# A gated block with a selective scan and a mixture of experts: the stage up to the first scan rearranged

## The reference

```
x    : (4, 256, 256)   ctx : (4, 256, 128)   E = 8 experts, top 2, M = 512
# part 1: a selective state space model, DI = 256 channels, DS = 16 states, DR = 8
xi    = in_proj_w @ ctx                       # per batch, channels x time
xc    = depthwise causal convolution, 4 taps, of xi;   u = silu(xc + conv_b)
x_dbl = x_proj_w @ u  -> dt_lo (8 rows), B (16 rows), C (16 rows)
delta = softplus(dt_proj_w @ dt_lo + dt_proj_b);       A = -exp(A_log)
state = state * exp(delta * A) + (delta * u) * B ;     y = sum over states(state * C) + D * u
y     = y * silu(layernorm(x))                # layernorm(x)[channel, time] stands as z
x     = x + tanh(g_xattn) * transpose(y)
# part 2: routed mixture of experts on 1024 tokens
x     = x + tanh(g_ffn) * moe(layernorm(x))   # softmax over the best two of 8 logits
```

## Time and profile before

| | |
|---|---|
| median of 3 runs | 315.19 us (313.74 to 315.58) |
| the profiled execution | 316.63 us, its span 314.9 us |
| busy in the span | PE 266.2, DVE 230.8, ACT 179.8, POOL 177.5 us |
| first scan begins | 39.81 us into the span |
| last scan ends, routing, first expert product | 161.2, then to 189.5 us |
| mean granted TensorE clock | 0.92 |

### The profile page before, as it was taken

One profiled execution on the slowest core, in us unless ns is written; L12 is line 12 of the kernel. 1 busy time (PEld: TensorE's weight loads), 2 busy tenths in 40 slices (PEclk: granted clock), 3 DMA queues, 4 the chain that ended last, 5 costly groups with the idle time before them and its releaser, 6 DMA issues.

```text
span 314.9 us, 4621 instructions
## 1 busy us (share of the span) xinstructions
PE 266.2 (85%) x1139; PEld 176.7 (56%) x1140; DVE 230.8 (73%) x423; ACT 179.8 (57%) x335; POOL 177.5 (56%) x159
## 2 busy tenths in 40 slices
PE   3957569869977998898799398999999999999970
PEld 3522133224332533463547276889889898898860
DVE  2775997999889999999887993565655656556540
ACT  1396477767566677557482852474564655646540
POOL 5000337997899899999675033246455464554331
PEclk9988558999999999999879857999999999999985
DMA  6599400000000000001069511042332432423312
GB/s 199 184 370 387 153 1 0 0 3 0 0 0 1 0 3 0 0 0 68 2 200 323 210 37 34 17 69 39 63 59 41 67 47 53 67 35 65 35 18 33
DMA packets 18911, 22.70 MB, mean 72 GB/s; under 512 B 2624, under 2 KB 14062, under 8 KB 18894
## 3 DMA queue, kind: packets, MB, share of 16 engines
q1 hardware_dynamic: 13312, 16.39, 15.1%
q0 software_dynamic: 4416, 6.03, 12.0%
q10 hardware_dynamic: 1166, 0.08, 0.2%
HBM read 17.38 MB, written 5.11 MB: 71 GB/s over the span
## 4 chain that ended last, share of the span: by engine, by line
PE 58%; DVE 19%; issue 9%; POOL 4%; ACT 4%; DMA 3%; POOLq 1%; SPq 0%; DVEq 0%; ACTq 0%
PE PZ L976 11%; PE PD L940 11%; PE PU L940 10%; PE PY L779 10%; DVE states L1116 5%; DVE states L1122 4%; POOL hC L403 3%; PE PY L962 3%; DMA xs<-in_x 3%; PE PU L768 2%; DVE W_lo L1213 2%; PE PY L738 2%; PE PZ L933 1%; PE PU L917 1%; PE PZ L827 1%
## 5 line engine op out<-in xcount | busy, mean ns | idle before, releaser
L403 POOL TENSOR_TENSOR hC<-states,WO 128x512 f32<-128x512 f32 x64 | 80.8, 1274 | 21.8 <-PE PY L779 14.7
L1122 DVE TENSOR_TENSOR_SCAN states<-PD,states 128x512 f32<-128x512 f32 x64 | 77.4, 1210 | 1.0 <-ACT PD L577 1.0
L779 PE MATMUL PY<-hC,ident 128*128 128x512 f32 x128 | 71.2, 644 | 6.0 <-POOL hC L403 5.9
L438 POOL DMA_INDIRECT out<-lg,y_at x23 | 36.4, 1584 | 54.5 <-ACT lg L670 49.0
L577 ACT ACTIVATE PD<-WO,Aneg 128x510 f32<-128x510 f32 x64 | 43.9, 689 | 22.2 <-DVE states L1122 18.0
L1359 DVE TENSOR_TENSOR WO_lo<-WO,WO_hi 128x512 fp32r<-128x512 f32 x46 | 29.8, 688 | 34.5 <-ACT WO_hi L663 33.9
L663 ACT ACTIVATE WO_hi<-WO 128x512 fp32r x46 | 26.5, 624 | 48.5 <-PE PZ L976 46.8
L1116 DVE TENSOR_TENSOR states<-PU,WO 128x512 f32<-128x512 f32 x64 | 42.8, 670 | 4.8 <-POOL hC L403 3.1
L425 POOL DMA_INDIRECT hC<-x_rows,x_at x23 | 23.2, 1008 | 27.2 <-DVE x_at L1329 14.9
L779 PEld LDWEIGHTS PY<-hC,ident 128*128 128x128 f32 x128 | 23.0, 200 | 22.4 <-POOL hC L403 15.6
L394 POOL TENSOR_TENSOR W_lo<-W,W_hi 128x512 fp32r<-128x512 f32 x23 | 29.2, 1275 | 0.0
(11 more groups left out here) (226 smaller groups left out, 509.7 us busy)
## 6 DMA issues: line engine op xcount, KB each, us to landing
W<-in_L_ffn_w SPq DMA_DIRECT2D x16, 512.0 KB, 10.9
WO<-in_L_ffn_wo SPq DMA_DIRECT2D x8, 512.0 KB, 5.7
xs<-in_x SPq DMA_DIRECT2D x1, 1024.0 KB, 8.3
out<-xs SPq DMA_DIRECT2D x2, 512.0 KB, 3.3
x_rows<-u SPq DMA_DIRECT2D x2, 512.0 KB, 5.3
early<-in_ctx SPq DMA_DIRECT2D x1, 512.0 KB, 4.3
hC<-x_rows,x_at POOLq DMA_INDIRECT x23, 2.8
out<-lg,y_at POOLq DMA_INDIRECT x23, 3.8
```

The lines of the kernel that those rows point to most:

```text
L403: pool.tensor_tensor(hC[:, n % 2, :], states[:, n % RING, :], C_rep[:, pair % C_RING, :], ALU.mult).then_inc(hc_done, 1)
L438: pool.indirect_dma_start(out=out, out_offset=bass.IndirectOffsetOnAxis(ap=y_at[:, s:s + 1], axis=0), in_=y_tile[s % 2], in_offset=None, c ...
L779: pe.matmul(PY[:, h, :], ident[:, :], hC[:, n % 2, :], start=False, stop=(m == DS - 1)).then_inc(y_done, 1)
L1122: dve.tensor_tensor_scan(states[:, n % RING, :], DEC[n % 2], states[:, n % RING, :], 0.0, ALU.mult, ALU.add).then_inc(scan_done, 1)
```

## The change

Five things, in one edit. The layout: batches' tokens and channels are loaded with two neighbouring rows per partition ("(p r)" and "(p h)" for "(r p)" and "(h p)"), so that DMAs have pieces twice as long; PE then reads and writes some operands with stride 2 (`x_cols`, `z_cols`, `x2`), and `cols` is loaded straight instead of being turned. x comes in two halves, statistics too. DMAs move between the SP and ACT queues; W1 is loaded whole before W0.

`u`: only quarter 1 (`CONV`) still has the four scaled products; quarters 0, 2 and 3 have one product (`channels`) and taps, whose first is ACT's (`start_taps`) and whose other three DVE's (`taps`). dt_proj is folded with the dt rows of x_proj into `dt_w` (two products with 8 rows), so that `delta_raw(c)` is two 128-row products from u itself, and no dt_lo is copied.

Roots are exp(-0.5 ln(var)) on ACT, with no Sqrt and no reciprocal. Eight products of the identity stand ahead of PE's first work. `silu_z` of the second half's four blocks moves behind the last scan.

The order: delta quarter 0 is finished first and scan 0 runs ahead of quarter 1's delta and du; `delta_raw(2)`, `x_dbl(1)`, `delta_raw(3)`, `rows_hi(1)` and `rows_lo(1)` move behind the first scans. Dropped lines that the new order replaces are left out below where the section above names them.

```diff
-        XI = [bank[i] for i in (2, 4)]
-        XD = [bank[i][0:BC_LO + 2 * DS, :] for i in (5, 4)]
+        XI = {(0, 0): bank[0], (1, 0): bank[2], (1, 1): bank[5]}
+        CONV = bank[1]
         DRAW = [bank[i] for i in (6, 7, 6, 7)]
...
+            sp.dma_start(ctx_sb.rearrange("p (b r) d -> p b r d", r=2), ctx_1024.rearrange("b (p r) d -> p b r d", p=P)).then_inc(ld["ctx"], 16)
...
-            def softplus_base(c):
-                pool.wait_ge(relu_ok, c + 1)
...
+            pool.wait_ge(relu_act, 1)
+            pool.wait_ge(rest_ok, 2)
+            pool.tensor_tensor(sp_relu[1], sp_relu[1], sp_rest[1], ALU.subtract).then_inc(base_pool, 1)
...
+            act.dma_start(convw[:, :, :], conv_w.rearrange("(p h) k -> p h k", p=P)).then_inc(ld["convw"], 16)
+            act.dma_start(xproj_sb[:, :], x_proj_w).then_inc(ld["small"], 16)
+            act.dma_start(dtw_sb[:, :, :], dt_proj_w.rearrange("(p h) r -> p h r", p=P)).then_inc(ld["small"], 16)
...
+            def start_taps(q, h):
+
+                act.wait_ge(xi_ps, 2 * q + h - (1 if q else 0) + 1)
+                act.activation(u[:, q, h, :], XI[q, h], ACT.Copy, scale=convw[:, h, DC - 1:DC]).then_inc(first_tap, 1)
...
+                act.wait_ge(stats_ok, (q + 1) * (2 * QBLK + 1))
...
+                act.wait_ge(ln_var, q + 1)
+                act.activation(rstd[:, 0, cut], std[:, 0, cut], ACT.Exp, scale=-0.5).then_inc(rstd_ok, 1)
...
+            start_taps(0, 0)
+            act.wait_ge(smallT_ps, 1)
+            act.activation(dtwT[:, :, :].rearrange("r h e -> r (h e)"), bank[3][0:DR, P:3 * P], ACT.Copy).then_inc(dtwT_ok, 1)
+            start_taps(1, 0)
+            root_first(0)
+            act.preload_act_table_set("silu_and_others")
+            start_taps(1, 1)
+            act.wait_ge(dt_w_made, 1)
+            act.activation(dt_w.rearrange("p h e -> p (h e)"), dt_w_ps, ACT.Copy).then_inc(dt_w_ok, 1)
             for h in range(2):
...
-            for i in range(2):
-                silu_z(i)
             silu_u(0)
-            for i in range(2, 7):
-                silu_z(i)
-            for c in range(1, 2 * NQ):
-                silu_u(c)
-            silu_z(7)
-            act.preload_act_table_set("natural_log_exp_and_others")
-            act.wait_ge(ld["small"], 16 * 7)
-            act.activation(Aneg[:, :, :], Aneg[:, :, :], ACT.Exp).then_inc(Aexp_ok, 1)
+            act.wait_ge(nmr_ok, 1)
+            silu_z(0)
+            silu_z(1)
+            silu_u(1)
+            silu_z(2)
+            silu_z(3)
+            silu_u(2)
+            silu_u(3)
+            act.wait_ge(ld["gates"], 32)
+            act.activation(tg[:, :], gates[:, :], ACT.Tanh).then_inc(tanh_ok, 1)
...
+                    if n == ROOT_AT:
+                        root(0)
...
+                act.activation(std[:, 1, cut], vare[:, 1, cut], ACT.Ln).then_inc(ln_var2, 1)
+                act.wait_ge(ln_var2, q + 1)
+                act.activation(rstd[:, 1, cut], std[:, 1, cut], ACT.Exp, scale=-0.5).then_inc(rstd2_ok, 1)
...
+            act.preload_act_table_set("natural_log_exp_and_others")
+            magnitude(0)
+            exponent(0)
+            logarithm(0)
             rows_hi(0)
-            rows_hi(1)
-            magnitude(0)
+            act.wait_ge(ld["A"], 16)
+            act.activation(Aneg[:, :, :], Aneg[:, :, :], ACT.Exp).then_inc(Aexp_ok, 1)
             magnitude(1)
-            exponent(0)
             exponent(1)
-            logarithm(0)
-            logarithm(1)
             act.wait_ge(Aneg_ok, 1)
             act.wait_ge(dec_clear, 2)
-            decay(0, 2)
+            decay(0, 1)
+            positive(1)
+            logarithm(1)
+            decay(1, 2)
+            rows_hi(1)
+            root_first(1)
+            decay(2, 3)
             positive(2)
-            decay(2, 3)
-            positive(3)
             decay(3, 4)
             magnitude(2)
             decay(4, 5)
-            magnitude(3)
-            decay(5, 6)
             exponent(2)
             plus_one(2)
-            decay(6, 8)
+            decay(5, 9)
+            logarithm(2)
+            positive(3)
+            decay(9, 10)
+            magnitude(3)
+            decay(10, 12)
             exponent(3)
             plus_one(3)
-            decay(8, 11)
-            logarithm(2)
-            decay(11, 13)
+            decay(12, 16)
             logarithm(3)
-            decay(13, NT)
+            decay(16, NT)
             act.wait_ge(exp_done, NT)
...
+            act.preload_act_table_set("silu_and_others")
+            for i in (QBLK, QBLK + 2, QBLK + 1, QBLK + 3):
+                silu_z(i)
+            act.preload_act_table_set("natural_log_exp_and_others")
             act.wait_ge(b_ps, NT // 2)
...
+            pe.wait_ge(consts, 2)
+            for _ in range(8):
+                pe.matmul(bank[3][:, 0:P], ident[:, :], ident[:, :], start=True, stop=True)
...
+            pe.wait_ge(tapw_ok, DC)
...
+            pe.wait_ge(ctxT_ok, 2)
+            channels(0, 0)
+            pe.wait_ge(ctxT_act, 1)
+            channels(1, 0)
+            pe.wait_ge(ld["small"], 16 * 2)
             for h in range(2):
-                pe.wait_ge(tapw_ok, DC * (h + 1))
-                for k in range(DC):
...
+            channels(1, 1)
+            pe.wait_ge(dtwT_ok, 1)
...
-            def delta_raw(q):
-
-                pe.wait_ge(dt_ok, q + 1)
+            def delta_raw(c):
...
+                q, to = divmod(c, 2)
                 for h in range(2):
-                    if q:
-                        pe.wait_ge(abs_ok, h + 1)
-                    pe.matmul(DRAW[2 * q + h], dtwT[:, h, :], dt_lo[:, q, :], start=True, stop=True).then_inc(draw_ps, 1)
-
-            pe.wait_ge(small_ok, 4)
-            pe.wait_ge(u_ok, 2)
+                    pe.wait_ge(u_ok, 2 * q + h + 1)
+                    mm = pe.matmul(DRAW[c], dt_w[:, h, to * P:(to + 1) * P], u[:, q, h, :], start=(h == 0), stop=(h == 1))
+                mm.then_inc(draw_ps, 1)
+
+            pe.wait_ge(dt_w_ok, 1)
+            delta_raw(0)
+            pe.wait_ge(small_ok, 3)
             x_dbl(0)
-            pe.wait_ge(u_ok, 4)
-            x_dbl(1)
-            delta_raw(0)
+            delta_raw(1)
...
+                x2 = PZ[r][:, :].rearrange("p (l e h) -> p l h e", l=2, h=2)
...
-                        at = l * DX + h * P
-                        mm = pe.matmul(PZ[r][:, at:at + P], zs[:, q * QBLK + 2 * r + h, l * P:(l + 1) * P], scaled_id[:, :], start=False, stop=(l == 1 and h == 1))
+                        mm = pe.matmul(x2[:, l, h, :], z_cols[:, q * QBLK + 2 * r + h, l, :], scaled_id[:, :], start=False, stop=(l == 1 and h == 1))
...
             spread_B(0)
+            pe.wait_ge(gc_ok, 1)
             spread_C(0)
+            pe.wait_ge(relu_ok, 1)
+            pe.wait_ge(abs_ok, 1)
+            delta_raw(2)
             spread_B(1)
-            delta_raw(1)
+            pe.wait_ge(relu_act, 1)
+            pe.wait_ge(abs_ok, 2)
+            x_dbl(1)
             spread_C(1)
             spread_B(2)
-            through(0, SUM_AT[0] + 1)
+            through(0, RAW_AT)
+            pe.wait_ge(bc_lo, 2)
+            delta_raw(3)
+            through(RAW_AT, SUM_AT[0] + 1)
...
+            first_stats(0)
+            taps(0, 0)
+            first_mean(0)
+            taps(1, 0)
+            taps(1, 1)
...
+            def delta_sum(c):
+
+                dve.wait_ge(sp_ln_ok, c + 1)
...
+                dve.tensor_tensor(delta[c], sp_relu[c], sp_ln[c], ALU.add).then_inc(delta_ok, 1)
+
+            def drive_input(c):
+
+                dve.wait_ge(delta_ok, c + 1)
+                dve.tensor_tensor(du[c], delta[c], u[:, c // 2, c % 2, :], ALU.mult).then_inc(du_ok, 1)
+
             relu(0)
-            relu(1)
+            first_stats(1)
+            for i in range(2):
+                dve.memset(DEC[i].rearrange("p (b l) -> p b l", b=QB)[:, :, 0:1], 0.0).then_inc(dec_clear, 1)
+            rounding(0)
+            dve.wait_ge(rest_ok, 1)
+            dve.tensor_tensor(sp_relu[0], sp_relu[0], sp_rest[0], ALU.subtract).then_inc(base_ok, 1)
+            delta_sum(0)
             rows_lo(0)
             dve.wait_ge(Aexp_ok, 1)
             dve.tensor_scalar(Aneg[:, :, :], Aneg[:, :, :], -1.0, None, ALU.mult).then_inc(Aneg_ok, 1)
-            rows_lo(1)
...
+            centred_gate()
+            drive_input(0)
             rounding(1)
-            delta_and_du(dve, 0)
-            delta_and_du(dve, 1)
...
             drive(0)
-            through(0, 9)
+            scan(0)
+            delta_sum(1)
+            drive_input(1)
+            drive(1)
+            through(1, LOW_AT)
+            rows_lo(1)
+            first_mean(1)
+            through(LOW_AT, 8)
             rounding(2)
-            through(9, 11)
+            through(8, 14)
             rounding(3)
-            through(11, GATE_AT[0])
```

(43 more changed lines are left out.)

260 lines of the change are left out of this document (111 added, 149 removed).

## The result

The changed kernel takes 309.89 us (median of 4 runs, 308.98 to 310.2), the kernel before 314.47 beside it (4 runs, 313.19 to 315.58): ratio 0.985, 95% interval 0.981 to 0.989. That is 4.6 us less; the forecast was 307.2, or 8.0 less, with a range of 305 to 310. The profiled execution takes 310.16 us, its span 308.3.

The account below looks back on a forecast made before the run. The stage before the first scan was bound by a chain of waits with no engine full, the scans by DVE. 316.6 less 7.8 at scan 16 and 0.2 for a reciprocal gave 308.6, or 307.2 as median; range 305 to 310.

Parts of the forecast that it names:

- ACT's list of 11.8 and 0.7 of waits, to 19.1: Before the first scan: ACT's own work, 11.8 us plus 0.7 of waits for PE, ends last, at 19.1 us.
- 9.7 us from Abs to scan 0: DVE and ACT alternate from Abs to the first scan for 9.7 us; scan 0 taken at 29.0 (28.2 to 31.5).
- 1.0 us for POOL beside `delta_sum(1)` and du: Before scan 1: POOL's `times_C` beside DVE's two-operand work adds 1.0 us; scan 1 at 34.5, scan 2 unmoved by it.
- Scan 2 at 37.1, by its exp, and that by `x_dbl(1)`: Scan 2 waits for its `exp`, behind PE's `x_dbl(1)`; 37.1 us (35.5 to 38.5) against 43.23, a gain of 6.1.
- 26.2 us from scan 2 to 16: Scans 2 to 16: steps, roundings, moved work and 0.3 of waits make 26.2 us against 27.9, 1.7 more gained.
- this just fits; 0 to 0.5 us: Behind the last `exp`: ACT's 3.3 us of deferred `silu_z` and table switches lie beside PE, costing 0 to 0.5 us.
- That one was 1.4 us above the median: Base of the sum: the profiled execution, 316.6 us, was 1.4 above the median, turning 308.6 into 307.2.
- (c): Router: stride 2 doubles PE's loads of weights, 4 us back, 311.1 us; chance 0.08.
- (e): Scans: PE stays at the low clock level and loses 1.3 us a pair; 333 us if held over 20 pairs; chance 0.03.
- (a): Ramp to the scans: PE chokes and stays low, scan 2 at 39.8, gain 2.9, 312.3 us; chance 0.13.
- (b): PE runs high from the start, slow stretch at the end goes too; scan 2 at 35.5, 302.5 us; chance 0.12.
- (d): Scans are full for ACT or POOL with the moved work, so all is given back; 314 us, within 1%; chance 0.04.

Follow-up runs that it names:

- second series: Both kernels timed and profiled again with no edit: before 314.41 us (profiled execution), changed kernel 310.02 us (6 runs), ratio 0.9847.
- silu_z_left_out: Changed kernel without the first half's four `silu_z` ahead of the first scan, POOL filling their tiles with ones: 308.91 us, one run.
- pool_hold: Changed kernel with POOL's first product with C waiting until both du are written: 310.06 us (309.5 to 311.35).
- second execution of before: The kernel before, unedited, profiled once more: 314.41 us, against 316.63 us in its first profile.
- second pair: Second profiles of both kernels, no edit: 314.41 us for the kernel before, 309.47 us for the changed kernel.

## Why the prediction was right or wrong

**Direction and range** held, the range by luck: 309.89 lies 0.1 us inside its upper bound of 310, the second series' 310.02 just outside, and the gain is 4.6 us for 8.0. The mechanism held up to scan 16 but for one wait, and missed behind the last scan. By its steps:

- **inwT's copy at 6.6**: 6.81. **ACT's list of 11.8 and 0.7 of waits, to 19.1**: Abs at 19.95, 13.1 us after the copy instead of 12.5; the waits were 1.2. The cause was right (silu_z_left_out), but PE is closer behind than thought: it ends last as soon as ACT's list is 1 us shorter, and without the warm-up products 0.7 is lost.
- **The second table load, 1.28 and nothing behind it**: 18.66 and 1.28, Abs at 19.95. Held.
- **9.7 us from Abs to scan 0**: 10.0, of which `first_stats(1)` 1.9 by its removal. Scan 0 29.96 for 29.0.
- **1.0 us for POOL beside `delta_sum(1)` and du**: 1.04 by the row, 1.0 at scan 1 by pool_hold. Its sign, du at 1.6, did not come: `delta_sum(1)` met POOL, and du took 0.69. The rule of the Trainium skill (SBUF — State Buffer, Who interferes with whom), that such a DVE operation and a GpSimd one that reads SBUF contend, holds here: 1.73 us beside POOL and 0.69 without it. But "scan 2 would not move" is wrong: scan 2 moved by the same 1.0.
- **Scan 2 at 37.1, by its exp, and that by `x_dbl(1)`**: 36.89, and the reason is wrong. `x_dbl(1)` ended at 32.6, near the 32.3 that I had for the high clock, and moving it changed nothing. Scan 2 follows scan 1, which is set by DVE's own work for quarter 1 behind a scan 0 that was 1 us late. Two errors met, PE quicker and DVE's chain longer, and the hit is luck.
- **26.2 us from scan 2 to 16**: 26.46. Gain at scan 16 7.8, as said, in this pair; 7.25 in the second, since this stretch of the kernel before also varies.
- **The end, "this just fits; 0 to 0.5 us"**: the term that failed; the sum took it at 0. From the last scan to the mask the second execution of before takes 8.2 us, the changed kernel 10.3 and 10.5. Of these 2.1 us or more, 1.5 came back with the roundings ahead; the rest goes with PE's clock over its last sums. I asked whether ACT's list fits beside PE, and it does; I did not ask what else waits for ACT's roundings (POOL), nor where POOL's work would then fall (on DVE's chain, a stall of the kind that I had priced at scan 1). The reciprocal's 0.2 is there: mask to expert 19.6 before, 19.4 after.
- **"That one was 1.4 us above the median"**: the base of the sum hid part of the loss. The first profile of before held the slow stretch of the earlier trace rows (29.5 us from last scan to first expert product, 27.8 in the second), and I subtracted from it as if the gain would be the same against an execution without it. Of the 3.4 us that were missing, the second pair puts about 0.7 at or before the last scan (7.1 instead of 7.8) and 2.1 between it and the first expert product, 2.3 if the reciprocal's 0.2 is counted; 0.4 more is between these two profiles and the medians.
- **Rivals.** (c) fell: the router's 16 instructions take 1.94 and 2.06 us with stride 2, 1.85 and 2.00 before. (e) and (a) fell: the clock was up at 40 us. (b) came half true: scan 2 near 36.9, and the slow stretch at the end was 5.39 us instead of 6.43 in the first pair, but its gain was covered by the wait for POOL ahead of the mask. It had priced that stretch at 2.8 us, which is PE's own time; at the CAST the two executions of before differ by 1.7 (9.3 and 7.6 us behind the last scan). And "brought on by 1.37 us of idle" is not borne out: the execution without the stretch has 1.38 us of idle at the same place. (d) fell: 7.1 us are kept at the last scan.
- **Its own signs.** 28 us from the last scan to the first expert product were forecast, 29.7 and 29.9 measured: this sign showed the failed term. The router's rows came to 2.06, over the 2 that were named, but they had been 2.00 before.

**Open.** What share POOL's hold has in the time. Why PE's eight turns take 1.04 to 1.97 us in executions of kernels whose head is the same up to there. And which of the five changes gave how much of the 9.9 us at scan 0: they were not undone one by one, but for scan 0's order and the eight products ahead.

## What to carry to other kernels

Work that is moved behind a stage is hidden only if its followers on other engines are hidden too: follow each signal of the engine it is moved onto, one engine further. Before you subtract from a profiled execution, look whether it holds a disturbance that the others may not have, and take a second profile if you can. And a stall of DVE on POOL is worth looking for again each time the order changes; here it cost 1.0 and 1.5 us in two places, and one went by a wait, the other by an order of instructions.
